# Moving the indirect transfers of four scans into their preparations on GpSimd, and the low parts of split weights from VectorE to GpSimd

## The reference, cut to what matters

```python
x = L0_attn_x                                             # 4 sequences x 512 x 256
x = x + 0.5 * ffn(layernorm(x), Wr, Wg, Wu, Wd)           # 64 experts, top 8 of them per token
x = x + attn(layernorm(x), Wx, Wz, WB, WC, Wdt, Wlam, Wth, A_log, ...)
x = x + 0.5 * ffn(layernorm(x), Wr, Wg, Wu, Wd)

def attn(x):          # 64 heads, state 128 x 8 per head
    B, C = rmsnorm(x @ WB.T) + B_bias, rmsnorm(x @ WC.T) + C_bias
    B, C = rope(B, cumsum(theta * dt)), rope(C, cumsum(theta * dt))     # theta = x @ Wth.T
    # scan over time: h = alpha*h + beta*B_prev*x_prev + gamma*B*x;  y = C.h
    return (y * silu(x @ Wz.T)) @ Wout.T

def ffn(x):
    w, idx = top_k(softmax(x @ Wr.T), 8);  w = w / sum(w)
    return sum over the 8 experts of  w * (silu(x @ Wg[e]) * (x @ Wu[e])) @ Wd[e]
```

## Time and profile before

| | |
|---|---|
| median of three runs | 3351.05 us |
| time of the profiled execution | 3350.67 us |
| its span | 3348.9 us |
| PE busy | 2812.7 us (84%) |
| DVE busy | 2403.5 us (72%) |
| ACT busy | 1820.8 us (54%) |
| POOL busy | 1587.4 us (47%) |
| mean granted TensorE clock | 0.913 |

### The profile page before, as it was taken

How to read it: one execution, slowest core, us unless ns; L and a number is a source line. 1 busy time by engine, 2 the same in 40 slices (tenths; PEclk the granted TensorE clock), 3 DMA queues, 4 the chain that set the end, 5 groups by cost and what they waited for, 6 DMA issues and landing times.

```text
span 3348.9 us, 84316 instructions
## 1 busy us (share of the span) xinstructions
PE 2812.7 (84%) x28752; PEld 2145.2 (64%) x28752; DVE 2403.5 (72%) x3926; ACT 1820.8 (54%) x3740; POOL 1587.4 (47%) x1420
## 2 busy tenths in 40 slices
PE   4359987888888899999985999998899999659980
PEld 3348874666666666666763677776577777448870
DVE  5333454999999569899955899995699999433454
ACT  1136645666666266666623777772677776136650
POOL 2750441555555335565610566663256666170356
PEclk7579998898999899999987999998999999779995
DMA  9967974665665256566502666662566664467883
GB/s 392 311 198 247 294 243 136 185 192 168 183 192 157 75 149 170 161 171 173 144 4 92 182 181 173 178 172 62 154 170 177 177 184 123 169 214 250 275 286 118
DMA packets 315371, 609.75 MB, mean 182 GB/s; under 512 B 59152, under 2 KB 163728, under 8 KB 314128
## 3 DMA queue, kind: packets, MB, share of 16 engines
q1 hardware_dynamic: 290576, 539.83, 53.1%
q0 software_dynamic: 24576, 67.14, 6.4%
...
## 4 chain that ended last, share of the span: by engine, by line
PE 48%; DVE 16%; issue 11%; DMA 10%; POOL 9%; ACT 4%; SPq 2%; DVEq 1%; POOLq 0%; ACTq 0%
PE bank L64 16%; POOL xd L494 6%; PE bank L573 5%; PE bank L1200 4%; PE bank L1330 3%; DVE tmp L1278 3%; DMA ykq<-yd,ic 3%; PE bank L1396 3%; PE bank L1394 2%; PE bank L1370 2%; DVE xbc L1254 2%; DVE rot L1278 2%; DMA xh<-xd 2%; PE bank L564 2%; PE cs_sn L587 2%
## 5 line engine op out<-in xcount | busy, mean ns | idle before, releaser
L64 PE MATMUL bank<-xh,wb 128*128 128x512 f32 x2048 | 680.3, 413 | 64.6 <-ACT btr L1345 35.0
L64 PEld LDWEIGHTS bank<-xh,wb 128*128 128x128 f32 x2048 | 370.2, 191 | 181.1 <-ACT btr L1345 55.0
L1209 ACT ACTIVATE xbc<-bank,norm_w 128x512 f32<-128x512 f32 x512 | 350.8, 685 | 236.3 <-PE bank L64 229.4
L1286 POOL TENSOR_TENSOR rot<-rot,tmp 128x512 f32<-128x512 f32 x256 | 340.4, 1330 | 199.2 <-DVE tmp L1278 199.2
L64 PE MATMUL bank<-xl,wb 128*128 128x512 f32 x1024 | 407.0, 397 | 0.0
L649 DVE TENSOR_TENSOR hh<-sg,bank 128x96 f32<-128x96 f32 x384 | 97.7, 254 | 389.9 <-ACT sg L623 388.8
L1287 POOL TENSOR_TENSOR rot<-rot,tmp 128x512 f32<-128x512 f32 x256 | 360.3, 1408 | 0.0
L1298 POOL TENSOR_TENSOR sq<-cst,rho 128x512 f32<-128x512 f32 x128 | 133.5, 1043 | 462.1 <-DVE x L1014 326.7
L1303 POOL TENSOR_TENSOR xc<-xc,sq 128x512 f32<-128x512 f32 x128 | 163.2, 1275 | 384.4 <-DVE xwp L1265 384.4
L1278 DVE SCALAR_TENSOR_TENSOR rot<-xbc,bias,cs_sn 128x1024 f32<-128x1024 f32 x256 | 325.4, 1271 | 8.4 <-DVE xbc L1254 6.7
L1278 DVE SCALAR_TENSOR_TENSOR tmp<-xbc,bias,cs_sn 128x1024 f32<-128x1024 f32 x256 | 326.4, 1275 | 0.0
...
## 6 DMA issues: line engine op xcount, KB each, us to landing
...
rr_bc<-rr_dram SPq DMA_DIRECT2D x128, 512.0 KB, 5.8
...
dt_bc<-row_dram SPq DMA_DIRECT2D x256, 128.0 KB
al_bc<-row_dram SPq DMA_DIRECT2D x256, 128.0 KB, 3.7
...
```

The costliest lines, as they stand in the source:

```text
L64: ins = e.matmul(dst, a, m, start=start and c == 0, stop=stop and c == n - 1, skip_group_check=not (start and stop))
L1209: e.activation(xbc[j % 4][:, i, :], of(i)[:, :], ACT.Copy, scale=norm_w[:, i:i + 1])
L1286: e.tensor_tensor(R[:, 2 * ty, :], R[:, 2 * ty, :], tmp[:, 2 * ty + 1, :], ALU.subtract)
```

## The change

1. In scans 0 and 1 GpSimd does all 32 gathers of the scan in `gather_prep_pool`, before it waits for `x1`: three transfers ahead, into four buffers `got`, each followed on GpSimd by a multiply with the routing weight (a tensor_scalar of 128x256) and an add into `acc4` (a tensor_tensor of 128x256). The memset of `acc4`, the turn's gather and DVE's L806 are gone.
2. In scans 2 and 3 GpSimd does all 32 scatters in `scatter_prep_pool`: an index copy, a copy of 128x256 from `keep` to `got`, the DMA. ACT's copy in the turn and the turn's scatter are gone.
3. In scan 0 GpSimd makes the low parts, at its turn's end behind `F_pool`, in the place of DVE. Those of the pairs before the turns stay on DVE.
4. The scatters of the FFN use four semaphores instead of two, and `combined` places the multiply-adds of the FFN in later blocks: 54 of the 64 stand in the block loop, before and after, from block 138 on instead of from block 120 on.

```diff
-        combined = lambda i: paced(i) + LATE
+        combined = lambda i: max(NRB + i, paced(i)) + LATE
...
+        def gather_prep_pool(e, b):
+            n, c, w = NP * b, RT * TOPK + NP * b, w8[:, :, :].rearrange("p t k -> p (t k)")
+            def row(i):
+                if n + i >= 4:
+                    e.wait_ge(e_gc.sem, e_gc.at(n + i - 3))
+                    e.nop(nofuse=True)
+                e.indirect_dma_start(got[i % 4][:, :], None, yd, bass.IndirectOffsetOnAxis(idx[:, c + i:c + i + 1], 0)).then_inc(a_gk[i % 4].sem, 16)
+            def add(i):
+                acc = acc4[:, i // TOPK, :]
+                e.wait_ge(a_gk[i % 4].sem, a_gk[i % 4].at((n + i) // 4 + 1))
+                e.nop(nofuse=True)
+                if i % TOPK == 0:
+                    e.tensor_scalar(acc, got[i % 4][:, :], w[:, c + i:c + i + 1], None, ALU.mult).then_inc(e_gc.sem, 1)
+                else:
+                    e.tensor_scalar(got[i % 4][:, :], got[i % 4][:, :], w[:, c + i:c + i + 1], None, ALU.mult).then_inc(e_gw.sem, 1)
+                    e.wait_ge(e_gw.sem, e_gw.at(n - n // TOPK + i - i // TOPK))
+                    e.wait_ge(e_gc.sem, e_gc.at(n + i))
+                    e.nop(nofuse=True)
+                    e.tensor_tensor(acc, acc, got[i % 4][:, :], ALU.add).then_inc(e_gc.sem, 1)
...
+            for i in range(3):
+                row(i)
+            for i in range(NP):
+                if i + 3 < NP:
+                    row(i + 3)
+                add(i)
...
+        def scatter_prep_pool(e, b):
+            n = (b - SG) * NP
+            for i in range(NP):
+                j = i % 4
+                e.wait_ge(a_sp[j].sem, a_sp[j].at(RT * TOPK // 4 + (b - SG) * (NP // 4) + i // 4))
+                e.nop(nofuse=True)
+                e.tensor_copy(ic[j][:, :], idx[:, bass.ds(n + i, 1)]).then_inc(e_ic.sem, 1)
+                e.tensor_copy(got[j][:, :], keep[:, bass.ds((b - SG) * TT + i // TOPK, 1), :].rearrange("p a d -> p (a d)")).then_inc(e_xst.sem, 1)
+                e.wait_ge(e_ic.sem, e_ic.at(n + i + 1))
+                e.nop(nofuse=True)
+                e.wait_ge(e_xst.sem, e_xst.at(n + i + 1))
+                e.nop(nofuse=True)
+                e.indirect_dma_start(xd[0:NRB * P, :], bass.IndirectOffsetOnAxis(ic[j][:, 0:1], 0), got[j][:, :], None).then_inc(a_sp[j].sem, 16)
...
+        def wb_low_pool(e, q, j):
+            e.wait_ge(e_wbs.sem, e_wbs.at(q))
+            e.nop(nofuse=True)
+            e.wait_ge(e_wbh.sem, e_wbh.at(q + 1))
+            e.nop(nofuse=True)
+            e.tensor_tensor(wb[j % 2][:, 1, :], wb_raw[:, :], wb[j % 2][:, 0, :].bitcast(F32), ALU.subtract).then_inc(e_wbs.sem, 1)
...
@@ turn_pool @@
                 D_pool(e, n, j)
-                if gathers(b):
-                    gather_turn_pool(e, b, n, q, j)
-                else:
-                    scatter_turn_pool(e, b, n, q, it, j)
                 if T:
...
                 F_pool(e, n, j, [0])
                 F_pool(e, n, j, [1])
+                if is_first(b) and not last:
+                    wb_low_pool(e, q + 4, j)
+                if is_first(b) and not (last and j >= 1):
+                    th_low_pool(e, q + 3, j + 1)
@@ turn_dve @@
-                if gathers(b):
-                    gather_turn_dve(e, b, n, q, it, j)
-                if is_first(b) and not last:
-                    wb_low_dve(e, q + 4, j)
-                if is_first(b) and not (last and j >= 1):
-                    th_low_dve(e, q + 3, j + 1)
@@ pairs_pool @@
             if gathers(b):
-                e.memset(acc4, 0.0).then_inc(e_az.sem, 1)
+                gather_prep_pool(e, b)
+            else:
+                scatter_prep_pool(e, b)
             e.wait_ge(e_x12.sem, e_x12.at(b + 1))
```

More of the change, by code:

```diff
@@ L118, in build @@
         keep = sb("keep", [P, RT, D])
-        ic = [sb(f"ic{i}", [P, 1], U32) for i in range(2)]
+        ic = [sb(f"ic{i}", [P, 1], U32) for i in range(4)]
         with ExitStack() as ffn_ctx:
@@ L177, in build @@
         wb_raw, th_raw = keep[:, 0:4, :].rearrange("p t d -> p (t d)"), sb("th_raw", [P, D])
-        acc4, ykq = keep[:, 4:8, :], sb("ykq", [P, D])
-        stage = [ykq, th_raw]
+        acc4 = keep[:, 4:8, :]
+        got = [sb(f"got{i}", [P, D]) for i in range(4)]
         wx_sb = xbc[3][:, 0:KD, :]
@@ L219, in build @@
         a_zf, a_sc = [arr(f"a_zf{i}") for i in range(NH2)], soft("a_sc")
-        a_sp = [soft(f"a_sp{i}") for i in range(2)]
+        a_sp = [soft(f"a_sp{i}") for i in range(4)]
         a_xg, a_wd, a_ys = ([arr(f"{n}{i}") for i in range(c)] for n, c in (("a_xg", NXG), ("a_wd", NWD), ("a_ys", NYS)))
@@ L482, in scattered @@
                 e.wait_ge(a_sc.sem, a_sc.at(RT * TOPK * (c + 1)))
-            for i in range(2 if h == 0 else 0):
-                e.wait_ge(a_sp[i].sem, a_sp[i].at(RT * TOPK // 2 * (c + 1)))
+            for i in range(4 if h == 0 else 0):
+                e.wait_ge(a_sp[i].sem, a_sp[i].at(RT * TOPK // 4 * (c + 1)))
         def scatter_pool(e, g, t):
@@ L493, in scatter_pool @@
                 c = (h * RT + t) * TOPK + k
-                e.indirect_dma_start(xd[0:NRB * P, :] if h == 0 else xd, bass.IndirectOffsetOnAxis(idx[:, c:c + 1], 0), xt[h][:, t, :], None).then_inc((a_sp[k % 2] if h == 0 else a_sc).sem, 16)
+                e.indirect_dma_start(xd[0:NRB * P, :] if h == 0 else xd, bass.IndirectOffsetOnAxis(idx[:, c:c + 1], 0), xt[h][:, t, :], None).then_inc((a_sp[k % 4] if h == 0 else a_sc).sem, 16)
         def gather_pool(e, g, t):
@@ L779, in ffn_sp @@
             blocks_sp(e, c)
-        e_gc, e_ic, e_az, e_tk, e_xst = (ev(n) for n in "e_gc e_ic e_az e_tk e_xst".split())
-        a_gk = soft("a_gk")
+        e_gc, e_gw, e_ic, e_tk, e_xst = (ev(n) for n in "e_gc e_gw e_ic e_tk e_xst".split())
+        a_gk = [soft(f"a_gk{i}") for i in range(4)]
         gathers = lambda b: isinstance(b, int)
[L785 to L806, removed]
+        def gather_prep_pool(e, b):
[17 more added lines that the diff above has]
+                    e.tensor_tensor(acc, acc, got[i % 4][:, :], ALU.add).then_inc(e_gc.sem, 1)
+            if b == 1:
+                e.wait_ge(e_tk.sem, e_tk.at(1))
+                e.nop(nofuse=True)
[5 more added lines that the diff above has]
+                add(i)
@@ L1056, in wb_high_act, with th_low_pool @@
             e.activation(wb[j % 2][:, 0, :], wb_raw[:, :], ACT.Copy).then_inc(e_wbh.sem, 1)
+        def wb_low_pool(e, q, j):
+            e.wait_ge(e_wbs.sem, e_wbs.at(q))
+            e.nop(nofuse=True)
+            e.wait_ge(e_wbh.sem, e_wbh.at(q + 1))
+            e.nop(nofuse=True)
+            e.tensor_tensor(wb[j % 2][:, 1, :], wb_raw[:, :], wb[j % 2][:, 0, :].bitcast(F32), ALU.subtract).then_inc(e_wbs.sem, 1)
+        def th_low_pool(e, q, j):
+            e.wait_ge(e_ths.sem, e_ths.at(q))
+            e.nop(nofuse=True)
+            e.wait_ge(e_thh.sem, e_thh.at(q + 1))
+            e.nop(nofuse=True)
+            e.tensor_tensor(th[j % 2][:, 1, :], th_raw[:, :], th[j % 2][:, 0, :].bitcast(F32), ALU.subtract).then_inc(e_ths.sem, 1)
         def wb_low_dve(e, q, j):
```

14 lines of the change are left out of this document (removed).

## The result

The changed kernel took 3437.43 us, the median of four runs (3433.92 to 3442.21), against 3351.56 us (3346.88 to 3356.59). The ratio is 1.0259, with a 95% interval of 1.0246 to 1.0272. The forecast was 3425 us. The profiled execution took 3436.94 us, 86.3 us more than that of before.

The account below looks back on a forecast made before the run. It took PE to bound scans 2 and 3 and DVE scan 0; from 3350.67 us, +11.3 + 16 (scan 0), +32.9 - 23.4 (scan 1), +17.3 + 17.3 and +3 made +74: 3425 us, own range 3400 to 3450.

Parts of the forecast that it names:

- The preparation on GpSimd, scans 0 and 1: 32 gathered blocks ahead of the turns outlast GpSimd's idle time: +11.3 us in scan 0, +32.9 us in scan 1.
- G: Length of the gather preparation on GpSimd in scans 0 and 1: 100 us, low ends 80, high ends 123.
- The preparation, scans 2 and 3: 32 scatters on GpSimd ahead of the turns: +17.3 us in each scan, with 0 counted for the turns.
- S: Length of the scatter preparation on GpSimd in scans 2 and 3: 82 us, low ends 69, high ends 96.
- Scan 1, turns: With L806 and its transfer wait gone, a turn falls from 15.16 to PE's 14.38 us: -23.4 us.
- Scan 0, turns: With low parts on GpSimd, a turn takes 18.5 us on the mean against 17.91: +16 us.
- the lock: In scan 0, GpSimd's tensor_tensor and two-input DVE instructions exclude each other; everything behind is 3.0 to 3.2 us late.
- the reciprocal's wait: In odd turns of scan 0, DVE waits 3.5 us for the reciprocal's input, since SP issues L1230 behind th's store.
- DVE loses 4.3 us of a turn: In scan 0, the three instructions taken from DVE cover 4.3 us; alone that brings DVE to about 13.6.
- the reciprocal is in time: Rival for scan 0: the lock holds but SP reaches L1230 earlier; pace 16.8, 3379 us; chance 0.17.
- PE's pace in scan 0: Rival: low parts on GpSimd hold nothing up and a turn is 14.38 us; 3314 us; chance 0.14.
- The guess of 0 to 12: What PE's longer stand before its first G_pe does to its clock: 3 us added over all scans.

Follow-up runs that it names:

- e4: The changed kernel without the multiply by the routing weight in 28 of the 32 gathered blocks of scans 0 and 1: 3376.09 us, ratio 1.0060.
- e1: The changed kernel with the low parts of scan 0 back on DVE, all else as changed: 3399.16 us, ratio 1.0131.
- e11: The kernel before with only the scatters of scans 2 and 3 moved into the preparation: 3382.80 us, ratio 1.0104.
- e10: The changed kernel with SP issuing the norms' transfer (L1253) ahead of th's store, in scan 0 alone: 3410.07 us, ratio 1.0185.

## Why the prediction was right or wrong, point by point

From the profiled executions, stretch by stretch (us):

| stretch | forecast | measured |
|---|---|---|
| first FFN | 0 | +1.6 |
| scan 0, first transfer to turn 2 | +11.3 | +33.7 |
| scan 0, turns 2 to 31 | +16 | -2.1 |
| scan 1, start | +32.9 | +48.2 |
| scan 1, turns 2 to 31 | -23.4 | -20.1 |
| scan 2, start and turns | +17.3 | +16.1 |
| scan 3, start and turns | +17.3 | +12.6 |
| clock, second FFN | +3 | -3.7 |
| sum | +74 | +86 |

The forecast of 3425 us is 12 under the measured 3437. That is closer than its terms are: the starts of scans 0 and 1 came out 38 us dearer, the turns of scan 0 18 us cheaper, the rest 8 us cheaper. That these cancel is luck.

**The preparation on GpSimd, scans 0 and 1: right in kind, a term mis-sized.** "The multiply of 128x256 ... I take 0.42"; it takes 0.94 (median of 56), above the upper bound of 0.63, which was half of a tensor_tensor of 512 columns. 32 x 0.52 = 16.6 us a scan, and G was 119.2 in scan 0 and 116.1 in scan 1 instead of 100. e4 shows it as the cause. The rest of the sum stood: wait 0.75, DMA 1.01, seam 0.17, add 0.72. The misses at the starts of scans 0 and 1, 22 and 15 us, are nearly all this term. Another 3 us in scan 0 are the stretch from L1377 to L1288 of turn 2, 21.2 us long (18.0 before). In it DVE waits for the input of the reciprocal:

```profile
630.90 0.35 DVE L1244 RECIPROCAL rc<-rc_in 128x32 f32<-128x32 f32 x1 [5.93 <-DMA rc_in<-decay_t]
```

Before, this wait was 1.84 us. In e1, where PE and DVE stand as long at the start but the low parts are on DVE, there is no such wait and the same stretch takes 16.0 us. So these 3 us belong to the low parts' move, not to the preparation.

The Trainium skill (GPSIMD Engine Reference, "Performance versus the Vector engine") gives 1.8 cycles an element as the best case, by which 256 elements are an estimated 0.38 us. The copy of this size took 0.40, and the trace agrees. The multiply with a scalar for each partition took 0.94, and there the measurement decides.

**The preparation, scans 2 and 3: right.** S was 78.2 against 82, and the turns gave nothing back, as "I count 0" had it (e11).

**Scan 1, turns: right.** 14.46 us, PE's pace.

**Scan 0, turns: the mechanism right, three terms mis-sized.** The turn of 18.5 us was built from a turn of scan 2, with the lock and the reciprocal's wait added; it measured 17.70.

- The lock was to put everything "3.0 to 3.2 us late". L1283 takes 3.18 us on the mean (1.20 before) and L1288 0.64 (0.35 before), 2.3 us together. In the even turns this is the whole miss, 15.4 us against 16.2.
- The reciprocal is late as forecast, but by 2.5 us in 10 of 13 odd turns against 3.5 in each: 0.98 us a turn against 1.75.
- DVE's waits for PE, (16.8 + 5.8) / 26 = 0.87 us a turn, were put at nothing. In the turn shown above, DVE's 3.15 us at 803.82 come behind PE's 3.40 for the squares and its stretch at 1.2 GHz.

The first two make the turn 0.8 us shorter each, and the third makes it 0.9 longer; with them the sum is 17.8.

One reading was wrong without touching that sum: "DVE loses 4.3 us of a turn". The durations in the earlier trace rows were not DVE's work: of wb low's 2.30 us 1.08 were a wait for GpSimd's rotations, and of th low's 1.50 about the same (its shortest is 0.42). So a turn without gathers was 16.25 us (e1), and not the 17.3 that a subtraction of L806 gives, and the low parts' move added 1.45 to it. The forecast compared its 18.5 with the 17.91 of before, and so did not see that the gathers' leaving had made room.

e10 shows that the late reciprocal is the larger part of the price. It nearly makes the rival "the reciprocal is in time": a turn of 16.69 us against its 16.8, and 3410 us against its 3379, of which the multiply is 33 (2 x 16.6).

**PE's pace in scan 0 (the rival below before): wrong** in every run with wb low on GpSimd: none was under 16.6 us.

**Clock.** PE stood 115 us before L1353 in the four scans together, and its clock was at 1.2 GHz at the end of it. What that cost behind the stand does not show: in scan 1 the stretch from the first rotation's end to L1288 of turn 2 takes 15.9 us, 16.6 before, and the 3 us in scan 0 have the other cause just named. The guess of 0 to 12 holds at its low end. What I did not see is the same within scan 0's turns: 3.4 us of standing, then over 10 us at 1.2 GHz.
